# Attention of layer 0: one output turn per two units, fills on GpSimd, the maxima's transpose four matmuls earlier

## What is computed

```python
q_c = (c_q @ Wq_up).reshape(b, s, N_HEADS, HEAD_DIM)      # head dim 4, latent 64
q_r = (x @ Wq_rope).reshape(b, s, N_HEADS, ROPE)          # 64
k_c = (c_kv @ Wk_up).reshape(b, s, N_HEADS, HEAD_DIM)
v_c = (c_kv @ Wv_up).reshape(b, s, N_HEADS, HEAD_DIM)
k_r = x @ Wk_rope
scores = (einsum('bqhd,bkhd->bhqk', q_c, k_c) + einsum('bqhd,bkd->bhqk', q_r, k_r)) / scale
attn = softmax(scores, axis=-1)
out = einsum('bhqk,bkhd->bqhd', attn, v_c).reshape(b, s, N_HEADS * HEAD_DIM) @ Wo
```

## Time and profile before

| | us |
|---|---|
| median of 3 runs | 2463.31 |
| the profiled execution's own time | 2466.67 |
| its span, first to last instruction | 2464.5 |
| first transpose of maxima (L640) in the loop's regular part | 126.6 |
| PE busy | 2415.5 |
| DVE busy | 1573.4 |
| ACT busy | 1381.7 |
| POOL busy | 1152.5 |

### The profile page before, as it was taken

How to read it: one execution, slowest core, us unless ns; L and a number is a source line. 1 busy time by engine, 2 the same in 40 slices (tenths; PEclk the granted TensorE clock), 3 DMA queues, 4 the chain that set the end, 5 groups by cost and what they waited for, 6 DMA issues and landing times. The chain is left out here.

```text
span 2464.5 us, 39978 instructions
## 1 busy us (share of the span) xinstructions
PE 2415.5 (98%) x12184; PEld 1809.4 (73%) x12184; DVE 1573.4 (64%) x3052; ACT 1381.7 (56%) x2171; POOL 1152.5 (47%) x1153
## 2 busy tenths in 40 slices
PE   7999999999999999999999899989999999999998
PEld 4677777777777777777776588867888888888876
DVE  7666666666666666666666523277658567576577
ACT  3677777777777777777777533234325334344252
POOL 1556565656565656565655344325234343343341
PEclk9999999999999999999999999999999999999999
DMA  6222222222222222222222322120010010000100
GB/s 219 43 46 54 46 54 46 55 46 54 46 54 46 55 46 54 52 47 54 46 54 51 118 90 88 54 86 18 26 43 17 26 43 17 26 25 17 39 1 35
DMA packets 49148, 125.40 MB, mean 51 GB/s; under 512 B 6801, under 2 KB 25233, under 8 KB 42962
## 3 DMA queue, kind: packets, MB, share of 16 engines
q1 hardware_dynamic: 49106, 124.85, 19.1%
HBM read 80.27 MB, written 10.49 MB: 37 GB/s over the span
## 5 line engine op out<-in xcount | busy, mean ns | idle before, releaser
L427 DVE TENSOR_REDUCE row_max<-ps_max 128x1 f32<-128x512 f32 x1024 | 670.7, 687 | 197.7 <-PE ps_max L517 179.0
L292 POOL TENSOR_TENSOR p_parts<-probs,p_parts 128x1024 f16<-128x1024 f32 x256 | 548.0, 2150 | 370.2 <-ACT p_parts L346 370.2
L341 ACT ACTIVATE probs<-ps_score 128x1024 f32<-128x1024 f32 x512 | 523.1, 1022 | 244.9 <-PE ps_score L533 219.4
L531 PE MATMUL ps_score<-Q,K 128*128 128x512 f32 x1024 | 409.1, 400 | 4.1 <-ACT probs L341 2.1
L533 PE MATMUL ps_score<-Q,K 97*128 97x512 f32 x1024 | 406.0, 396 | 0.0
L517 PE MATMUL ps_max<-KX,Q 68*128 68x512 f32 x1024 | 378.6, 411 | 3.3 <-DVE row_max L427 3.1
L421 DVE TENSOR_TENSOR Q<-ps_x,Q 64x512 fp32r<-64x512 f32 x254 | 175.0, 689 | 222.4 <-ACT Q L336 218.7
L346 ACT ACTIVATE p_parts<-probs 128x1024 f16<-128x1024 f32 x256 | 269.5, 1053 | 4.0
L531 PEld LDWEIGHTS ps_score<-Q,K 128*128 128x128 f32 x1024 | 194.4, 190 | 69.4 <-ACT probs L341 12.1
L517 PEld LDWEIGHTS ps_max<-KX,Q 68*128 68x128 f32 x1024 | 189.0, 189 | 76.2 <-issue 28.1
L533 PEld LDWEIGHTS ps_score<-Q,K 97*128 97x128 f32 x1024 | 195.0, 190 | 38.0
(11 more groups left out here) (289 smaller groups left out, 4232.7 us busy)
## 6 DMA issues: line engine op xcount, KB each, us to landing
Q<-Q SPq DMA_DIRECT2D x64, 512.0 KB, 4.3
ffn_raw<-in_w_ffn SPq DMA_DIRECT2D x22, 768.0 KB, 4.4
w_raw<-in_w_qrope SPq DMA_DIRECT2D x32, 512.0 KB, 3.7
wq_raw<-in_wq SPq DMA_DIRECT2D x8, 1024.0 KB, 5.6
wo_raw<-in_wo SPq DMA_DIRECT2D x8, 1024.0 KB, 4.9
content_k<-probs SPq DMA_DIRECT2D x8, 512.0 KB, 6.5
Q<-content_q SPq DMA_DIRECT2D x64, 64.0 KB
K<-content_k SPq DMA_DIRECT2D x64, 64.0 KB
```

The source lines that it names most:

```text
L292: pool.tensor_tensor(p_lo[:, j, :, :], probs[:, j, 0:PAIRED, :], p_hi[:, j, :, :], ALU.subtract)\
L341: act.activation(probs[:, j, 2 * half:2 * half + 2, :], ps_score[half][:, :, :], ACT.Exp, scale=SCALE).then_inc(exped, 1)
L427: dve.tensor_reduce(row_max[:, j * ST + t:j * ST + t + 1], ps_max[t % 2][:, :], axis=AXX, op=ALU.max)\
L531: pe.matmul(ps_score[half][:, k, :], K1[:, b, t * P:(t + 1) * P], Q1[:, b, j, :], start=True, stop=False)
```

## The change

The V tiles hold the values of batch 1 sixteen columns further right than those of batch 0. So in ps_o, of the 32 rows of a head, rows 0 to 12 belong to batch 0 and rows 16 to 28 to batch 1, and the `v` matmuls of both units of a group accumulate into the same ps_o. It is copied (`t`), transposed (`o` on PE) and normalised (`o` on DVE) once for each group, in the unit with b = 0 of the next group. Where a unit with b = 1 follows such a unit, its p0 waits for `o_made`; the other p0 only for `q_low`. T stands after p0 instead of after p1. The six fills are moved from DVE to POOL.

```diff
-            "p0 p1 T p2 v3 v2 v1 v0 m00 m01 s00 m02 q0 m03 m10 q1 q2 m11 "
+            "p0 T p1 p2 v3 v2 v1 v0 m00 m01 s00 m02 q0 m03 m10 q1 q2 m11 "
...
-                    return slot[:, b, :, :, 0:VP * HD0].rearrange("p t h (d k) -> p t h d k", k=VP)[:, :, :, :, k]
+                    return slot[:, b, :, :, 16 * b:16 * b + VP * HD0].rearrange("p t h (d k) -> p t h d k", k=VP)[:, :, :, :, k]
...
+            for b in range(NB):
+                for tile in (Q2, K2):
+                    pool.memset(tile[ROPE:P, b, :, :].bitcast(F32), 0.0).then_inc(zeros_set, 1)
+            pool.wait_ge(zeros_set, 2 * NB)
+            for b in range(NB):
+                pool.memset(K2[MROW:MROW + 1, b, :, :].bitcast(F32), 1.0).then_inc(zeros_set, 1)
+                pool.wait_ge(zeros_set, 2 * NB + b + 1)
...
-            def take_o(n):
-                act.wait_ge(pv_made, n + 1)
+            def take_o(g):
+                act.wait_ge(pv_made, 2 * g + 2)
...
-                        if kind == "t" and before:
-                            take_o(n - 1)
+                        if kind == "t" and before and b == 0:
+                            take_o(g - 1)
...
-            def normalise(g, b, n):
+            def normalise(g):
...
-                dve.wait_ge(r_made, 2 * n + 2)
-                dve.tensor_tensor(O[:, b * ST:(b + 1) * ST, bass.ds(g * GH * HD0, GH * HD0)].rearrange(
-                    "p t (h d) -> p t h d", h=GH), o_sum[:, :, :, :],
-                    recip[:, :, :, :].broadcast_to([P, ST, GH, HD0]), ALU.mult).then_inc(o_made, 1)
+                dve.wait_ge(r_made, 2 * g + 2)
+                for b in range(NB):
+                    ins = dve.tensor_tensor(O[:, b * ST:(b + 1) * ST, bass.ds(g * GH * HD0, GH * HD0)].rearrange(
+                        "p t (h d) -> p t h d", h=GH), o_sum[:, :, :, b, :],
+                        recip[:, :, :, b, :].broadcast_to([P, ST, GH, HD0]), ALU.mult)
+                ins.then_inc(o_made, 1)
...
-                        if kind == "o" and not (first and b == 0):
-                            normalise(g - 1 + b, 1 - b, n - 1)
+                        if kind == "o" and not first and b == 0:
+                            normalise(g - 1)
...
-                                if first:
+                                if first or b == 0:
                                     pe.wait_ge(q_low, 2 * n + 2)
                                 else:
-                                    pe.wait_ge(o_made, n - 1)
+                                    pe.wait_ge(o_made, g)
...
-                        if kind == "o" and before:
-                            if more:
-                                pe.wait_ge(q_low, 2 * n + 4)
-                            else:
-                                pe.wait_ge(o_made, n - 1)
-                            turn_o(n - 1)
+                        if kind == "o" and before and b == 0:
+                            pe.wait_ge(q_low, 2 * n + 4)
+                            turn_o(g - 1)
```

More of the change, by code:

```diff
@@ L62, in mla_stage @@
         v_rest = buf("v_rest", [P, PAIRED, GH, HD0])
-        o_sum = buf("o_sum", [P, ST, GH, HD0])
+        o_sum = buf("o_sum", [P, ST, GH, NB, HD0])
         row_max = buf("row_max", [P, GH * ST])
@@ L66, in mla_stage @@
         oT = buf("oT", [P, S])
[L67 removed]
+        recip = buf("recip", [P, ST, GH, NB, 1])
         V_slot, V_parts, V, O, ident = sb["V_slot"], sb["V_parts"], sb["V"], sb["X"], sb["ident"]
@@ L313, in _ @@
             for slot in (V_slot, V_parts):
-                pool.memset(slot[:, :, :, :, VP * HD0:VP * HD0 + 1], 1.0).then_inc(set_up, 1)
+                for b in range(NB):
+                    one = 16 * b + VP * HD0
+                    ins = pool.memset(slot[:, b, :, :, one:one + 1], 1.0)
+                ins.then_inc(set_up, 1)
             pool.memset(ident[:, :], 0.0).then_inc(set_up, 1)
@@ L413, in _ @@
             run(act, body)
-            take_o(2 * groups - 1)
+            take_o(groups - 1)
         @block.vector
@@ L447, in rope_keys @@
                    .then_inc(rope_low, 1)
[L449 to L453, removed]
-                dve.memset(K2[MROW:MROW + 1, b, :, :].bitcast(F32), 1.0).then_inc(zeros_set, 1)
             for c in range(DC):
@@ L486, in body @@
                             low(n + 1, 1 - b, 1)
-                        if kind == "o" and not (first and b == 0):
-                            normalise(g - 1 + b, 1 - b, n - 1)
+                        if kind == "o" and not first and b == 0:
+                            normalise(g - 1)
             run(dve, body)
-            normalise(groups - 1, 1, 2 * groups - 1)
-            dve.wait_ge(o_made, 2 * groups)
+            normalise(groups - 1)
+            dve.wait_ge(o_made, groups)
         @block.tensor
@@ L544, in outputs @@
                         pe.matmul(ps_o[32 * j:32 * (j + 1), :], V_slot[:, b, t - PAIRED, j, :], probs[:, j, t, :],
-                                  start=t == V_FIRST, stop=False)
+                                  start=t == V_FIRST and b == 0, stop=False)
                     return
@@ L551, in outputs, with turn_o @@
                         last = pe.matmul(ps_o[32 * j:32 * (j + 1), :], V_parts[:, b, t, j, :], part[:, j, t, :],
-                                         start=False, stop=t == V_LAST and part is p_lo)
+                                         start=False, stop=t == V_LAST and part is p_lo and b == 1)
                 if t == V_LAST:
                     last.then_inc(pv_made, 1)
-            def turn_o(n):
-                pe.wait_ge(o_taken, n + 1)
+            def turn_o(g):
+                pe.wait_ge(o_taken, g + 1)
                 for t in range(ST):
@@ L669, in _ @@
                 outputs(2 * groups - 1, 1, t)
-            pe.wait_ge(o_made, 2 * groups - 1)
-            turn_o(2 * groups - 1)
+            pe.wait_ge(o_made, groups - 1)
+            turn_o(groups - 1)
 EPS = 1e-5
```

11 lines of the change are left out of this document (6 added, 5 removed).

## The result

| us | before | after |
|---|---|---|
| median | 2461.87 (4 runs, 2459.85 to 2470.69) | 2649.70 (4 runs, 2641.07 to 2651.38) |
| ratio, 95% interval | | 1.0748 [1.0713, 1.0784] |
| span of the profiled execution (its own time 2650.35 after) | 2464.5 | 2648.2 |
| T of unit 1, and of unit 62 | 84.8 and 1326.4 | 83.4 and 1503.1 |
| mean unit, T to T, from unit 3 on | 20.34 | 23.29 |

The account below looks back on a forecast made before the run. PE was taken to bound the kernel, with DVE and ACT close to its path. +0.37 us a group over 31 groups (+11.5), -3.0 at the start and +0.4 at the end gave +8.9: 2472 us, range 2456 to 2484.

Parts of the forecast that it names:

- (a): T after p0 in the unit after a normalisation: normalisation +0.39 us (bounds 0.30 and 0.79), T late, +0.51 us of PE.
- second product +0.17: Part of the longer normalisation on DVE: one more product per group adds 0.17 us.
- (e): The start: without DVE's fills its splits begin earlier; -3.0 us, bounds -3.5 and 0, the latter if casts wait for fills.
- (d): Unit starting 0.51 us later: mrow's DMA nearly always in time, so a mean wait of 0.11 us goes once a group.
- (b): T after p0 in a unit that follows no normalisation: T waits for m33's reduction, +0.10 us.
- (c): The output's turn leaves every second unit, but m23 waits for DVE: -0.13 us, bounds 0 and 0.44.
- (f): The last normalisation, at the end of the stage with nothing beside it: +0.4 us.
- R3: Rival: normalisation at the upper bound, +0.79 us, T late by 1.04; 2484 us or a little over; chance 0.19.
- R1: Rival: PE's work is what counts, the turn's 0.44 us is won whole; 2447 us; chance 0.12.
- R2: Rival: mrow's DMA hides much of PE's delays at s00, 0.2 us a group; 2466 us; chance 0.18.
- R4: Rival: only the moved fills count and the group is neutral; 2460 us; chance 0.08.
- the T rows have no idle time before their weight loads: Sign in the profile after, at T on PE, that would show the prediction wrong; forecast waits some 0.4 and 0.2 us.

Follow-up runs that it names:

- b_twice: Kernel before with a second identical sum in front of the product, which so starts later: 2653.78 us.
- a_write: Kernel after with GpSimd's subtraction replaced by a fill of the same tile, which reads nothing: 2473.7 us.
- a_psum: Kernel after with the reciprocal written back into PSUM, so the product has one operand in SBUF: 2471.64 us, ratio 1.0023 to the kernel before.
- a_early: Kernel after with DVE's normalisation one reduction earlier, between m30 and m31, operands still in SBUF: 2472.34 us.
- a_half: Kernel after with each GpSimd subtraction cut in two halves: 2569.74 us.
- a_psum_told: a_psum with T back in its old place after p1: 2471.70 us, ratio 1.0027 to the kernel before.
- b_t: Kernel before with T after p0 and nothing else: 2468.81 us, ratio 1.0010 to the kernel before.
- b_fill: Kernel before with the six fills on GpSimd and nothing else: 2465.23 us, ratio 0.9982 to the kernel before.
- a_split: a_psum_told with the normalisation in two pieces, reciprocal and sum ahead of m30, products between m31 and m32: 2462.35 us, ratio 0.9978 to the kernel before.
- a_split_sbuf: a_split with the reciprocal in SBUF, so the product has two SBUF operands again: 2461.21 us.

## Why the prediction was wrong

**The step that failed is in (a): the length of the normalisation**, "second product +0.17", "Together +0.39; bounds 0.30 ... and 0.79". From the first reciprocal to the next reduction it is 4.92 us (453.78 - 448.86) where it was 0.79: +4.13, five times my upper bound. 3.84 of it are the two held products (4.07 for both, where one took 0.23), the rest the longer reciprocal and sum. I priced the products from the one row of before, and that row was of a product which started 0.06 us ahead of the subtraction. What would have shown it was at hand: my own working has the sum end 0.2 us later, and GpSimd's timeline, which I didn't hold beside DVE's, has the subtraction 0.06 behind the product. The bound was wrong by its method: "the whole of today's once more" scales work, and this is a wait for another engine's instruction.

The Trainium skill (SBUF — State Buffer, "Who interferes with whom") states just this: a DVE instruction with two SBUF inputs and a GpSimd instruction that reads SBUF exclude each other, and whichever starts first holds the other for its whole length. I had used that page for the casts of (e) and not for the product. For the DVE instruction the traces agree with it at each point: held behind a subtraction (2.02 us, b_twice), not held behind a fill (0.222, a_write), not with one operand in PSUM (0.220, a_psum), not when ahead (0.222, a_early), and for half as long behind half an instruction (1.02 and 1.19, a_half). The other direction no run here shows for this pair: before, the subtraction starts 0.06 to 0.08 behind a product with some 0.15 us left to run, and takes 2.16 us in the mean, only 0.02 more than one with no product beside it.

**What the held product cost.** By a_psum the held products cost 2649.70 - 2471.64 = 178 us. A group of two units takes 46.64 in the kernel after and 40.92 in a_psum: 5.73 us. 3.8 are PE's wait. The other 1.9 are the stretch at 1.2 GHz after it: from p0 to p2, eight matmuls and T, is 457.55 - 453.99 = 3.56 us, where nine spacings of 0.233 are 2.10. Over all such passes these nine take 3.69 us in the mean against 2.17 in a_psum, and p2's four 1.49 against 1.01: 2.0 us more together. That the low clock is a consequence is shown (it goes with the wait); how much the same wait would cost at a steady clock no run here measures. Nor did I foresee ACT: it sits idle 4.1 us in front of mrow, where in the earlier trace rows it had no gap.

**The rest of (a) to (d)**, as a_psum shows it without held products. "About 20.7 for a unit with b = 0 and 20.3 for the other": 20.79 and 20.13. My sum for a group was +0.37; it is 40.92 - 40.67 = +0.24 (20.37 and 20.30 before). (a): the b = 0 unit grew by 0.42, forecast 0.51. The sum's +0.20 and the reciprocal's, forecast +0.02, were +0.20 and +0.10. (b), +0.10 for T waiting in a unit without normalisation, is there but is given back. Behind such a unit the way from p0 to p2 takes 1.99 us in a_psum and 1.89 in a_psum_told, where T doesn't wait, and p2's four matmuls, which in a_psum T no longer stands in front of, 1.01 against 1.11. I had put that gain at nothing. So b_t gives 20.31 for b = 1 as before, a_psum and a_psum_told 20.13 and 20.12; T's place is worth 0.01 there. (c), -0.13 from bounds of 0 and 0.44: a_psum and a_psum_told have 20.13 and 20.12 against 20.30, -0.18. (d) can't be read apart from the others. "Had T stayed, p0's would be the price" of 0.20 a b = 0 unit: 0.30 in a_psum_told. So the arithmetic of delays held to about 0.1 us a term. a_psum, which computes the same with one operand elsewhere, came at +4.3 us where +8.9 was forecast: inside the range, at about half of the forecast.

**(e), the start, -3.0.** DVE, then GpSimd, in the kernel after, to hold against the earlier trace rows and against 0.69 for a cast in the kernel before:

```profile
4.97 1.85 DVE L463 CAST xh<-p_parts 128x1024 fp32r<-128x1024 f32 x1 [4.97 <-DMA p_parts<-in_xT]
6.85 1.23 DVE L465 TENSOR_TENSOR xl<-p_parts,xh 128x1024 fp32r<-128x1024 f32 x1
8.05 1.06 DVE L463 CAST xh<-p_parts 128x1024 fp32r<-128x1024 f32 x1
...
17.22 0.69 DVE L469 TENSOR_TENSOR Q<-ps_score,X 128x512 fp32r<-128x512 f32 x1 [2.27 <-ACT X L375]
...
4.47 1.80 POOL L325 MEMSET K<- 64x2048 f32 x1
6.22 2.34 POOL L325 MEMSET Q<- 64x2048 f32 x1
8.51 2.34 POOL L325 MEMSET K<- 64x2048 f32 x1
```

Casts and fills do hold each other, as the Trainium skill says for a cast in a two-port mode (SBUF — State Buffer, "Who interferes with whom"): the fill at 4.47 ends at 6.27, the cast that began at 4.97 ends 0.55 after it, at 6.82, and the next fill, 0.54 longer than one alone, ends with it delayed. The second cast began at 8.05, 0.51 before a fill ended (8.56), and again ends 0.55 after. So a cast waits for the rest of the fill, and the first met the longest rest, 1.30 us: 5.1 us for the four instead of 2.8, 2.4 us lost. "By that rule four casts could each wait for a fill, some 2 us each" was too much, and -3.0 nearly right: the first low part starts at 17.22 instead of 21.31, and T of unit 0 comes at 52.23 instead of 53.98, between 51.1 and 51.8 in a_psum, a_write and b_fill. But T of unit 1 comes at 83.4 instead of 84.8, because the clock, at 1.2 GHz for part of this stretch in every trace, has a mean of 0.67 from 43.5 to 85 after, 0.79 before and 0.92 in a_psum. This differs from trace to trace without a rule that I can show: T of unit 1 comes anywhere from 73.8 us (a_psum, a_split) to 84.3 (a_split_sbuf), so the time of a single run can move 10 us by this alone. By whole times (b_fill) the fills on GpSimd gain 2 to 4 us.

**(f)**, +0.4 at the end, is too small to be seen.

**The rivals.** R3 had the right instruction, a normalisation longer than forecast, but made T wait where p0 did, and its price was fourteen times too small (0.40 a group more, where it was 5.73). R1 and R2 fall with the measured a_psum: b = 1 units gained 0.18 and not 0.44, and the b = 0 units' delay arrives in the period. R4 needs a neutral group, and a_psum's isn't (+0.24). The view that I should have read is the one nobody waits in: GpSimd's timeline beside the instruction whose start I was about to move. Of the signs that I named for a wrong prediction, "the T rows have no idle time before their weight loads" came true where it mattered: in the passes with a held product T's weight load waits for no reduction, because PE had waited at p0. My text said "the wait of p0 for `o_made` lies inside this"; it was the wrong one of the two. In the other units of the kernel after T's weight load does wait for DVE, 0.29 us each, and in a_psum 0.36 and 0.29, near the "some 0.4" and "some 0.2" of the prediction.

## What to carry to other kernels

Before an instruction of DVE with two SBUF operands is moved or delayed, look at what GpSimd runs at that time: 0.2 us later can cost 2 us, because the instruction that starts second waits for the first one's end, and its duration in the trace before tells nothing on that. Where the order can't be ensured, put one operand in PSUM, cut the GpSimd instruction, or move the DVE instruction ahead of it. A long DVE instruction that idles PE can be paid for a second time, since PE may come back at the lower clock: here 3.8 us of waiting brought 1.9 more.

## What had not been expected of the hardware

- A product of 128x64 takes 0.22 us when it starts 0.06 us ahead of a GpSimd subtraction of 2.15 us, and 2.02 us when it starts 0.18 behind it; GpSimd's instruction takes 2.16 us in the mean beside the first, 2.12 beside the products held in the kernel after, and 2.15 with none beside it.
- A held product is listed with its whole wait as busy time: DVE's busy time rose by 105 us with 70 instructions fewer.
- Within 3.80 us without a matmul the granted clock fell to 0.5, in all 30 passes, and stayed there for 3.4 or 6.8 us; with 1.9 us (a_half) it fell in 27 of 30 passes, for 3.4 us; in a_early, where PE waited 10.5 us in all for DVE (31 times, 3.0 us at the most), its mean over the same part was 1.00.
- A DVE cast of 128x1024 (0.69 us alone) ended 0.55 us after the fill that it ran beside, whether it had begun 1.30 or 0.51 us before that fill's end, and the next fill took 0.54 us more.
